# All edge tiles sorted by source block, rows picked by one-hot products, target one-hots made on GpSimd

## The chip, the core and the metric

The kernel runs on one core of one Trainium2 chip. That core has a matrix engine (TensorE, PE in the profile), VectorE (DVE), ScalarE (ACT), GpSimd (POOL), SyncE (SP), which here only starts transfers, and 16 DMA engines. The metric is the device time of one execution in microseconds. The kernel before took 4575.59 us (median of 3 runs, 4570.17 to 4577.93).

## The reference

A graph network on 2500 nodes of 128 features and 82,500 edges, which come sorted by target (`dst`). Six layers of the first kind, cut to what matters:

```
for l in range(6):
    W   = ssp(edge_attr @ mlp_w1[l] + mlp_b1[l]) @ mlp_w2[l] + mlp_b2[l]   # per edge, 100 -> 128 -> 128
    W   = W * C[:, None]                                                  # cosine cutoff of the edge
    xf  = h @ conv_w1[l]                                                  # per node
    msg = xf[src] * W                                                     # row of the edge's source
    agg = segment_sum(msg, dst, num_segments=N)
    x2  = agg @ conv_w2[l] + conv_b2[l]
    h   = h + (ssp(x2) @ lin_w[l] + lin_b[l])
```

Then a layer norm, three layers of the second kind (`agg = segment_sum(h[src], dst)`, then two small products on the nodes), and a layer norm. Everything is float32. `ssp` is softplus minus log 2.

## The kernel before

**Steps.** The edge work goes in groups of 4 tiles of 128 edges, 512 edges a group. One group is one step of the edge loop. A layer has 7 iterations of 24 steps, 168 steps, so the six layers have 1008. In step `i` TensorE runs the first product of group `i` (512 columns into `ps_h`), then the second product of group `i-2` (into `ps_w`), and the aggregation of group `i-4` (into `ps_a`). The groups `i`, `i-2` and `i-4` are thus in the pipe at the same time. ScalarE does exp and log of the first product (`xc`) and fills `ps_w` with the bias (`seed`). VectorE finishes ssp (`hid`), multiplies `ps_w` with the source rows (`message`, written to `ex_msg`), and adds the aggregate into `aggT` (`add_window`).

**Where the source rows come from.** There are two kinds of group. Of every 4 steps, 3 are plain: GpSimd starts 4 indirect DMAs (`gather_group`, one for each tile of 128 rows, from `node_table` in DRAM into `rows`), up to 8 steps ahead. The fourth is permuted: its edges were sorted by source block (20 blocks of 125 nodes) before the layers, so that each tile takes its rows from one block. Its rows come from a product of a 128x128 one-hot (`select`, loaded by DMA) with the block of the node table kept in SBUF (`table`, which shares its space with `hi_mid`). `select_rows` makes that product into `ps_g`, ScalarE copies it to `picked`.

**The target side.** In a plain group the 4 tiles are sorted by target and lie in a window of 32 nodes: one 128x32 one-hot a tile (`hot`), one 128x32 sum and one add. In a permuted group each tile has its own window of 128 nodes: 128x128 one-hots (`phot`, made on VectorE) and four adds, one after the other.

**Counts.** Beside this, VectorE and TensorE count edges by (source, target) for the second kind of layer: 16 count tiles an iteration, placed by `COUNT_STEP`.

**Before the layers.** `rec` holds the records (104 floats an edge) of the 148 tiles that are to be permuted. VectorE computes each edge's place, GpSimd scatters each tile with one indirect DMA into `permuted`, which SyncE has cleared. Then 42 groups are read back, turned by TensorE and written as `attr_permuted` and `src_select`; VectorE makes the 128x128 source one-hots for that (`xc`). The layers start when all are turned.

**After each layer's edges** the last node chunks are updated (`late_chunks`; 3 of the 5 chunks are updated early, within the iterations of `EARLY_AT`), the new table is stored to DRAM, and the next layer starts.

Each engine has its own instruction stream, and semaphores tie them. The order is written out by hand in the loops below.

Of the kernel before, what the change touches and what calls it, by code (L numbers as in the profile page):

```python
# [23 lines left out]
P = 128  # L24
# [9 lines left out]
U = 24  # L34
J = U // M
NIT = 7
BLK = 125
BLOCKS = -(-N // BLK)
NP_GROUPS = NIT * J
NQ_GROUPS = NIT * J * (M - 1)  # L40
REAL = -(-E // GE)
PT = NP_GROUPS * TPG
RT = PT - BLOCKS
QT = -(-E // P) - RT
assert QT <= NQ_GROUPS * TPG
AS, RS = M, 6
assert J * (M - 1) % RS == 0
# [6 lines left out]
EACH = -(-E // P)  # L54
CLEARS, REC_LOADS = 7, 4
REC_STARTS = [c * RT // REC_LOADS for c in range(REC_LOADS)]
# [13 lines left out]
PAD = 2 * TPG  # L70
AHEAD = NCH
LEAD = M
PRIME = 2

EARLY_AT = [3, 5, 6]
EARLY = len(EARLY_AT)
ADD_LAG = 6
COUNT_MAX = 255
LOW = P
RANK_BLOCKS = 3  # L80
# [5 lines left out]
LN_EPS = 1e-5  # L86

# [7 lines left out]
COUNT_STEP = [4, 4, 5, 6, 8, 9, 10, 11, 13, 13, 14, 15, 17, 18, 19, 20]  # L95
# [3 lines left out]
def use_of(u):  # L99
    return u // M * (M - 1) + u % M - 1  # L100


def gathers_of(g):
    return max(0, min(TPG, QT - g * TPG))


def permuted(u):
    return u % M == 0


def gnn_program(nc, xT_d, srcc_d, dst_d, plan_d, ew_d, attr_d, rec_d, edge_w_d, b2_d, first_w_d, node_w_d, gin_w_d,
# [5 lines left out]
    attrp_d = nc.dram_tensor("attr_permuted", [NP_GROUPS, G1, GE], f32, kind="Internal").ap()  # L117
    select_d = nc.dram_tensor("src_select", [NP_GROUPS, P, GE], f32, kind="Internal").ap()
    table_d = [nc.dram_tensor(f"node_table{i}", [NP, F], f32, kind="Internal").ap() for i in range(2)]

    with ExitStack() as ctx:
# [20 lines left out]
        iota = sb("iota", [P, NB * WIN + 1], i16)  # L142
# [18 lines left out]
        cut = sb("cut", [P, NG * TPG])  # L161
        base_f = sb("base_f", [P, NG])
        base_i = sb("base_i", [P, LEAD + NG], i32)
        pbase_f = sb("pbase_f", [P, PT])
        pbase_i = sb("pbase_i", [P, PAD + PT], i32)
        block_i = sb("block_i", [P, PAD + PT], i32)
# [14 lines left out]
        src_all = sb("src_all", [P, NG * TPG], i32)  # L181

        scratch = counts[:, :, :].rearrange("p b n -> p (b n)").bitcast(f32)
        dst_i, src_part, len_raw, len_mask = (scratch[:, i * NG * TPG:(i + 1) * NG * TPG] for i in range(4))
        dst_i, src_part = dst_i.bitcast(i32), src_part.bitcast(i32)
        ends, ends_all, span = (scratch[:, (4 * TPG + 2 * i) * NG:(4 * TPG + min(2 * i + 2, 5)) * NG] for i in range(3))

        TABLES, ALL = (4 * TPG + 5) * NG, (NB + 1) * NCOL // 2
# [4 lines left out]

        rec, at = after(TABLES, RT * REC)
        total, at = after(at, BLOCKS * RT)
# [8 lines left out]
        bucket_shift, at = after(at, BLOCKS)  # L204
        pos_f, at = after(at, RT)
        pos_i, at = after(at, RT)
        slot_i, at = after(at, RT)
        tile_i, at = after(at, RT)
        slot_i, tile_i = slot_i.bitcast(i32), tile_i.bitcast(i32)
        assert at <= ALL  # L210
        rec = rec.rearrange("p (t r) -> p t r", r=REC)
# [4 lines left out]
        bucket = table[:, 0:BLOCKS * RT // 2].bitcast(bf16)  # L216
        src_low = sb("src_low", [P, NG * TPG], i16)
# [16 lines left out]
        buffers = sb("buffers", [P, AS + 2, GE])  # L234
        attr = buffers[0:G1, 0:AS]
        select = buffers[:, AS:AS + 2]
        xT = buffers[:, 0:NCH, :].rearrange("p c n -> p (c n)")
        spare = buffers[:, :, :].rearrange("p c n -> p (c n)")
        above, spare_at = spare[:, 0:(BLOCKS + 1) * RT // 2].bitcast(bf16), (BLOCKS + 1) * RT // 2
# [19 lines left out]
        ex, msg = ex_msg[:, 0:2, :], ex_msg[:, 2:4, :]  # L259

        stage_one, step_one = ex[:, 0, :], ex[:, 1, :]
        hid = sb("hid", [P, 3, GE])
        lg = msg
        picked = hid[:, 2, :]
        kept_attr = [ex[:, 0, :], ex[:, 1, :], buffers[:, 0, :], buffers[:, 1, :]]
# [1494 lines left out]
```

## Time and profile before

| what | value |
|---|---|
| time, median of 3 runs without the profiler | 4575.59 us |
| the profiled execution, from its first to its last instruction (its span; no other time is recorded for it) | 6617.0 us |
| PE busy in the span | 72% |
| PEld, DVE, ACT, POOL busy | 54%, 46%, 33%, 45% |
| mean granted TensorE clock | 0.778 of full speed |
| mean DMA rate | 87 GB/s |
| start of the first `hid`, and of the last one | 376.3 us, 6296.5 us |

"Busy" sums instruction durations by engine. PEld is the loading of weights, which overlaps PE. The granted clock is either full (2.4 GHz) or half (1.2 GHz). "remote" and "another core or an unknown queue" stand for a wait whose end no recorded event explains. The profiled execution is 2041 us longer than the median of the runs.

### The profile page before, as it was taken

To read this page: it belongs to the slowest core of one execution; us is meant where nothing else is said; L and a number is where in the kernel's file an instruction comes from. 1 tells how busy PE (TensorE), PEld (TensorE's weight loads), DVE (VectorE), ACT (ScalarE), POOL (GpSimd) and SP (SyncE) were. 2 spreads that over 40 slices of the span, in tenths; PEclk is the share of its full clock that TensorE was granted. 3 is DMA by queue.
4 is the path that set the end of the run, shared out by engine and by line. 5 is a ranking of instruction groups with operands and counts; after the bars stand their busy time and mean duration, and the time that the engine had idled before them with its cause. 6 is when DMAs were issued, how large, how long until landed. Compare 5 with 4: busy or idle time off the path is not lost.

```text
span 6617.0 us, 88816 instructions
## 1 busy us (share of the span) xinstructions
PE 4785.2 (72%) x24401; PEld 3558.4 (54%) x24684; DVE 3028.4 (46%) x8117; ACT 2174.5 (33%) x3585; POOL 2995.9 (45%) x3161
## 2 busy tenths in 40 slices
PE   0376777867777777777777777767777777777789
PEld 0365555645555555555555555545555555555544
DVE  3244444544444444444444444544444444444532
ACT  0133333333333333333333333333333333333322
POOL 5634444444454445444445444444445444445400
PEclk5687777777777777777777777777778777777799
DMA  4452233233233333233333323233333332323300
GB/s 157 137 151 84 83 86 88 82 91 85 82 87 85 85 90 89 80 86 86 86 86 91 85 84 88 85 85 87 85 85 88 86 89 84 86 84 87 87 14 9
DMA packets 324938, 574.64 MB, mean 87 GB/s; under 512 B 73578, under 2 KB 117300, under 8 KB 322996
## 3 DMA queue, kind: packets, MB, share of 16 engines
q1 hardware_dynamic: 202572, 357.07, 17.9%
q0 software_dynamic: 100160, 203.51, 11.5%
q10 hardware_dynamic: 21928, 11.64, 0.6%
q14 instruction: 261, 2.14, 0.1%
q8 instruction: 17, 0.28, 0.0%
HBM read 524.00 MB, written 47.93 MB: 86 GB/s over the span
## 4 chain that ended last, share of the span: by engine, by line
PE 40%; another core or an unknown queue 27%; issue 13%; DVE 10%; DVEq 4%; ACT 4%; POOL 2%; DMA 1%; ACTq 0%; SPq 0%; POOLq 0%
PE ps_w L680 10%; PE ps_h L781 9%; PE ps_a L695 8%; PE ps_a L692 4%; PE ps_pair L894 3%; POOL permuted L551 2%; DVE ex_msg L1428 2%; PE ps_pair L707 2%; DVEq L342 2%; ACT ps_w L1025 1%; DVE aggT L1409 1%; PE ps_a L669 1%; DVE phot L1388 1%; ACT xc L1062 1%
## 5 line engine op out<-in xcount | busy, mean ns | idle before, releaser
L561 POOL DMA_INDIRECT rows<-node_table,src_all x2982 | 2820.5, 946 | 3117.5 <-DVE ex_msg L1428 1937.8
L680 PEld LDWEIGHTS ps_w<-edge_w,hid 128*128 128x128 f32 x8064 | 1336.7, 242 | 1295.6 <-issue 1295.3
L680 PE MATMUL ps_w<-edge_w,hid 128*128 128x128 f32 x8064 | 1392.8, 329 | 719.0 <-ACT ps_w L1025 471.4
L1571 DVE SCALAR_TENSOR_TENSOR hid<-xc,ps_h 128x512 f32<-128x512 f32 x1008 | 690.9, 686 | 1859.5 <-remote 1328.5
L1060 ACT ACTIVATE xc<-ps_h 128x512 f32<-128x512 f32 x1008 | 601.3, 597 | 2648.2 <-remote 1363.6
L781 PE MATMUL ps_h<-buffers,edge_w 112*128 112x512 f32 x2016 | 1347.9, 756 | 86.4 <-DVE hid L1571 46.3
L695 PE MATMUL ps_a<-hot,ex_msg 128*128 128x32 f32 x6048 | 952.1, 306 | 469.7 <-issue 251.2
L695 PEld LDWEIGHTS ps_a<-hot,ex_msg 128*128 128x128 f32 x6048 | 887.8, 226 | 522.6 <-issue 512.8
L1062 ACT ACTIVATE xc<-xc,half_col 128x512 f32<-128x512 f32 x1008 | 727.3, 722 | 32.6
L1025 ACT COPY ps_w<-seed_rows 128x512 f32<-128x512 f32 x1008 | 591.6, 587 | 413.9 <-DVE ex_msg L1428 342.8
L1416 DVE TENSOR_TENSOR aggT<-aggT,ps_a 128x32 f32 x756 | 140.4, 186 | 927.2 <-remote 631.0
L1428 DVE TENSOR_TENSOR ex_msg<-ps_w,rows 128x512 f32<-128x512 f32 x756 | 518.6, 686 | 0.7
L692 PE MATMUL ps_a<-phot,ex_msg 128*128 128x128 f32 x2016 | 384.7, 351 | 110.0 <-DVE aggT L1416 103.5
L781 PEld LDWEIGHTS ps_h<-buffers,edge_w 112*128 112x128 f32 x2016 | 378.8, 231 | 117.8 <-issue 111.2
L692 PEld LDWEIGHTS ps_a<-phot,ex_msg 128*128 128x128 f32 x2016 | 344.6, 258 | 122.8 <-issue 118.8
L1409 DVE TENSOR_TENSOR aggT<-aggT,ps_a 128x128 f32 x1008 | 290.5, 288 | 209.3 <-issue 64.5
L707 PE MATMUL ps_pair<-pair_hot,low_hot 128*128 128x128 bf16 (+1 forms) x1092 | 284.3, 329 | 114.9 <-DVE pair_hot L1478 48.8
L669 PEld LDWEIGHTS ps_a<-hi_mid,buffers 128*128 128x128 f32 x2016 | 267.7, 193 | 128.4 <-issue 128.4
L1021 ACT COPY hid<-ps_a 128x512 f32<-128x512 f32 x252 | 144.9, 575 | 564.0 <-remote 545.4
L1388 DVE TENSOR_SCALAR phot<-pwin_now,prel_now,pcut_now 128x128 f32<-128x128 f32 x1008 | 283.5, 349 | 0.2
L669 PE MATMUL ps_a<-hi_mid,buffers 128*128 x2016 | 269.8, 277 | 5.2 <-DMA hi_mid<-node_table 3.2
L1478 DVE TENSOR_SCALAR pair_hot<-iota,pair_count 128x640 bf16<-128x640 int16 x672 | 270.2, 402 | 0.0
(236 smaller groups left out, 2825.5 us busy)
## 6 DMA issues: line engine op xcount, KB each, us to landing
buffers<-in_attr SPq DMA_DIRECT2D x756, 224.0 KB
buffers<-src_select SPq DMA_DIRECT2D x252, 256.0 KB
buffers<-attr_permuted SPq DMA_DIRECT2D x252, 224.0 KB
rows<-node_table,src_all POOLq DMA_INDIRECT x2982
permuted<-aggT SPq DMA_DIRECT2D x7, 1248.0 KB, 17.6
hid<-permuted SPq DMA_DIRECT2D x42, 208.0 KB
counts<-in_rec SPq DMA_DIRECT2D x4, 1924.0 KB, 35.4
hi_mid<-node_table SPq DMA_DIRECT2D x6, 1280.0 KB
```

The costliest lines, as they stand in the source:

```text
L561: pool.indirect_dma_start(out=rows[:, use % RS, t * F:(t + 1) * F], out_offset=None, in_=table[:, :], in_offset=bass.IndirectOffsetOnAxis( ...
L669: mm = pe.matmul(ps_g[:, t * F:(t + 1) * F], select[:, u // M % 2, t * P:(t + 1) * P], table[:, bass.ds(starts[t], F)], start=True, stop=True)
L680: mm = pe.matmul(ps_w[u % 2][:, t * F:(t + 1) * F], hid[:, u % 2, t * P:(t + 1) * P], edge_w[:, EW_W2:EW_W2 + F], start=False, stop=(t == ...
L692: mm = pe.matmul(ps_a[:, t * PWIN:(t + 1) * PWIN], msg[:, u % 2, t * F:(t + 1) * F], phot[:, t, :], start=True, stop=True)
L695: mm = pe.matmul(ps_a[:, 0:WIN], msg[:, u % 2, t * F:(t + 1) * F], hot[:, (u % M - 1) * TPG + t, :], start=(t == 0), stop=(t == TPG - 1))
L707: pe.matmul(ps_c[:, first:end], low_hot[:, q % 2, :], pair_hot[:, q % 2, first:end], start=(t == 0), stop=(t == TPG - 1), skip_group_check ...
L781: pe.matmul(ps_h[i % 2][:, :], edge_w[0:G1, EW_W1:EW_W1 + F], attr[:, i % AS, :], start=True, stop=True).then_inc(mm1_done[i % M], 1)
L1025: act.copy(ps_w[v % 2][:, :].rearrange("p (t f) -> p t f", f=F), seed_rows[:, :].unsqueeze(1).broadcast_to([P, TPG, F])).then_inc(seeded[v ...
L1060: act.activation(xc[:, u % 2, :], ps_h[u % 2][:, :], ACT.Exp).then_inc(exp_done, 1)
L1062: act.activation(xc[:, u % 2, :], xc[:, u % 2, :], ACT.Ln, bias=half_col[:, :]).then_inc(log_done[u % M], 1)
L1428: dve.tensor_tensor(msg[:, u % 2, :], ps_w[u % 2][:, :], gathered, ALU.mult).then_inc(msg_done[u % M], 1)
L1571: dve.scalar_tensor_tensor(out=hid[:, i % 2, :], in0=xc[:, i % 2, :], scalar=LOG_MAX, in1=ps_h[i % 2][:, :], op0=ALU.min, op1=ALU.max).the ...
```

## The change

All 645 tiles of 128 edges are now permuted, in three chunks of the target-sorted list (217, 213 and 215 tiles). In each chunk the tiles are sorted by source block, with room for the blocks' last, part-filled tiles: 704 tile slots, 176 groups. A layer is 11 iterations of 16 steps, 176 steps, 1056 in all.

- Every step has a `select_rows` product, a ScalarE copy to `picked` (now two buffers), four 128-node windows and four adds. No indirect DMA is left in the layers; `rows`, `hot`, `rel_now` and `cut_now` are gone.
- The one-hots `phot` (now two buffers) are made by GpSimd, 4 `tensor_scalar` a step, and so are the slices `prel_now` and `pcut_now`.
- SyncE loads `attr` (224 KB) and `select` (256 KB) for every step, 4 buffers each. The node table comes in 5 pieces.
- Before the layers the scatter runs over 645 tiles in 24 parts with 3 record buffers; chunk 1 is turned while chunk 2 is scattered, chunk 2 while chunk 3 is, and chunk 3 after the scatter. 176 groups are turned instead of 42, and `permuted` is cleared in 3 times 13 transfers.
- There are 12 count tiles an iteration instead of 16.

The order on VectorE, one step with its message, around a step without count tiles. Before, the message of a permuted group follows the making of its one-hots, and the adds of a plain group are one:

```order
L1563 UNCONDITIONAL_BRANCH
L1388 TENSOR_SCALAR phot<-pwin_now,prel_now,pcut_now 128x128 x4
L1428 TENSOR_TENSOR ex_msg<-ps_w,hid 128x512
L1571 SCALAR_TENSOR_TENSOR hid<-xc,ps_h 128x512
L1563 COMPARE_AND_BRANCH
L342 ISA
L342 TENSOR_LOAD base_i
L1416 ISA
L1416 TENSOR_TENSOR aggT<-aggT,ps_a 128x32
```

Now (`starts` holds the window starts; the message's rows in `hid` are `picked`):

```order
L336 TENSOR_LOAD starts
L1460 ISA
L1460 TENSOR_TENSOR aggT<-aggT,ps_a 128x128
L1460 ISA
L1460 TENSOR_TENSOR aggT<-aggT,ps_a 128x128
L1460 ISA
L1460 TENSOR_TENSOR aggT<-aggT,ps_a 128x128
L1460 ISA
L1460 TENSOR_TENSOR aggT<-aggT,ps_a 128x128
L393 REGISTER_ALU
L1467 TENSOR_TENSOR ex_msg<-ps_w,hid 128x512
L1599 SCALAR_TENSOR_TENSOR hid<-xc,ps_h 128x512
```

The one-hots have left VectorE, and every step has four 128-column adds.

The order on GpSimd inside the edge loop. Before, gathers alone:

```order
L386 ISA
L561 DMA rows<-node_table,src_all 128x128 x12
L386 REGISTER_ALU
L561 DMA rows<-node_table,src_all 128x128 x8
```

Now, one iteration of 16 steps (its first rows are the slices):

```order
L607 COPY prel_now<-prel 128x64
L608 REGISTER_ALU
L608 COPY pcut_now<-pcut 128x64
L609 ISA
L390 ISA
L592 ISA
L592 TENSOR_SCALAR phot<-pwin_now,prel_now,pcut_now 128x128 x8
L390 REGISTER_ALU
L592 TENSOR_SCALAR phot<-pwin_now,prel_now,pcut_now 128x128 x16
```

The stream of indirect DMAs is replaced by 64 `tensor_scalar` an iteration.

The order on TensorE before, two steps of plain groups with one permuted pick between (`ps_a<-hi_mid,buffers` is the pick from the table):

```order
L781 MATMUL ps_h<-buffers,edge_w 128x512
L680 MATMUL ps_w<-edge_w,hid 128x128 x4
L695 MATMUL ps_a<-hot,ex_msg 128x32 x4
L386 REGISTER_ALU
L781 MATMUL ps_h<-buffers,edge_w 128x512
L337 ISA
L337 TENSOR_LOAD block_i
L404 ISA
L669 ISA
L669 MATMUL ps_a<-hi_mid,buffers 128x128
```

Now, the end of one step and the start of the next:

```order
L709 MATMUL ps_a<-phot,ex_msg 128x128 x4
L813 UNCONDITIONAL_BRANCH
L399 REGISTER_ALU
L795 MATMUL ps_h<-buffers,edge_w 128x512
L336 ISA
L336 TENSOR_LOAD starts
L393 REGISTER_ALU
L689 ISA
L689 MATMUL ps_a<-hi_mid,buffers 128x128
```

The pick stands in every step, and every aggregation is of the wide form.

The diff, cut to its core:

```diff
-U = 24
+U = 16
-NIT = 7
+NIT = 11
+CHUNKS = 3
+CHUNK_GROUPS = [59, 58, 59]
+PARTS, RING = 8, 3
-COUNT_STEP = [4, 4, 5, 6, 8, 9, 10, 11, 13, 13, 14, 15, 17, 18, 19, 20]
+COUNT_STEP = [4, 4, 5, 6, 7, 8, 9, 10, 11, 12, 13, 13]
...
-            for t in range(RT):
-                if t in REC_STARTS:
-                    pool.wait_ge(rec_set, REC_STARTS.index(t) + 2)
-                    pool.sem_inc(gate, 1)
-                pool.indirect_dma_start(
...
+            for r in range(CHUNKS * PARTS):
+                if r % PARTS == 0:
+                    pool.wait_ge(places_set, r // PARTS + 1)
+                    pool.wait_ge(perm_clear, (r // PARTS + 1) * CLEARS * 16)
+                pool.wait_ge(rec_set, r + 1)
+                pool.sem_inc(gate, 1)
+                for t in range(PART_FIRST[r], PART_FIRST[r + 1]):
+                    pool.indirect_dma_start(
+                        out=perm_d[:, :], out_offset=bass.IndirectOffsetOnAxis(ap=pos_i[:, t:t + 1], axis=0),
+                        in_=rec[:, r % RING, t - PART_FIRST[r], :], in_offset=None).then_inc(scattered[r % RING], 16)
...
+            def match(uses, u):
+                uses.wait(agg_done, u - 2)
+                pool.sem_inc(gate, 1)
+                for t in range(TPG):
+                    op = pool.tensor_scalar(phot[:, u % 2, t, :], pwin_now[:, :], prel_now[:, u * TPG + t:u * TPG + t + 1],
+                                            pcut_now[:, u * TPG + t:u * TPG + t + 1], ALU.is_equal, ALU.mult)
+                op.then_inc(phot_done, 1)
...
-                if permuted(u):
-                    select_rows(uses, it, u, layer)
+                select_rows(uses, it, u, layer)
...
                 uses.wait(msg_done, u)
-                if u % M == 1:
-                    uses.wait_permuted(hot_done, u)
+                uses.wait_step(phot_done, u)
                 uses.wait(add_done, u - 1)
                 for t in range(TPG):
-                    if permuted(u):
-                        mm = pe.matmul(ps_a[:, t * PWIN:(t + 1) * PWIN], msg[:, u % 2, t * F:(t + 1) * F], phot[:, t, :],
-                                       start=True, stop=True)
-                    else:
-                        mm = pe.matmul(ps_a[:, 0:WIN], msg[:, u % 2, t * F:(t + 1) * F], hot[:, (u % M - 1) * TPG + t, :],
-                                       start=(t == 0), stop=(t == TPG - 1))
+                    mm = pe.matmul(ps_a[:, t * PWIN:(t + 1) * PWIN], msg[:, u % 2, t * F:(t + 1) * F], phot[:, u % 2, t, :],
+                                   start=True, stop=True)
...
+            def message(uses, u):
+
                 uses.wait(mm2_done, u)
...
+                uses.wait_step(picked_done, u)
+                dve.tensor_tensor(msg[:, u % 2, :], ps_w[u % 2][:, :], picked[:, u % 2, :], ALU.mult
+                                  ).then_inc(msg_done[u % M], 1)
...
+            find_places(0)
+            set_cuts()
+            fill_records(0)
+            fill_records(1)
+            find_blocks(0)
+            fill_records(2)
+            find_places(1)
+            find_blocks(1)
...
+            for r in range(PARTS, CHUNKS * PARTS):
+                fill_records(r)
+                for g in turned_after(r):
+                    turn_group(g)
```

## Rows read from the trace of the kernel before

**Rows 1.** Groups by line on GpSimd (busy us, mean ns of one | idle before, releasers)

```profile
L561 POOL DMA_INDIRECT rows<-node_table,src_all x2982 | 2820.5, 946 | 3117.5 <-DVE ex_msg L1428 1937.8 <-issue 1179.6
L571 POOL PARTITION_ALL_REDUCE buffers<-rows x1 | 1.3, 1291 | 71.1 <-DVE rows L1350 71.1
L539 POOL MEMSET mean_mat<- 128x128 f32 x1 | 0.2, 195 | 0.0
```

**Rows 2.** Timeline of GpSimd: a run of gathers, and the layer's end (start, duration)

```profile
1306.70 0.94 POOL L561 DMA_INDIRECT rows<-node_table,src_all  x1 [0.78 <-DVE ex_msg L1428]
...
1353.87 0.94 POOL L561 DMA_INDIRECT rows<-node_table,src_all  x1 [46.23 <-issue]
...
1371.34 0.94 POOL L561 DMA_INDIRECT rows<-node_table,src_all  x1 [0.30 <-issue]
```

**Rows 3.** One line each: gathers, scatter (ns min/median/max, first and last start)

```profile
L561 POOL DMA_INDIRECT rows<-node_table,src_all x2982: 938/944/1119, 267.6 to 6276.8; - x199
...
L551 POOL DMA_INDIRECT permuted<-counts x148: 954/958/4226, 48.3 to 240.1; - x148
```

**Rows 4.** Waits (engine and line, waited for: us in total, times, longest)

```profile
DVE hid L1571 <- remote: 1328.5, 240, 19.9
```

**Rows 5.** Timeline of VectorE from the layer's last gather (1306.70) to its last `hid`

```profile
1309.89 0.69 DVE L1571 SCALAR_TENSOR_TENSOR hid<-xc,ps_h 128x512 f32<-128x512 f32 x1 [0.51 <-ACT xc L1062]
...
1326.29 0.68 DVE L1571 SCALAR_TENSOR_TENSOR hid<-xc,ps_h 128x512 f32<-128x512 f32 x1
...
1354.01 1.29 DVE L1571 SCALAR_TENSOR_TENSOR hid<-xc,ps_h 128x512 f32<-128x512 f32 x2 [0.89 <-issue]
```

**Rows 6.** Timeline of TensorE: a full-clock step with pick and one count tile

```profile
2395.63 1.10 PE L781 MATMUL ps_h<-buffers,edge_w 112*128 112x512 f32 x2
2396.57 1.05 PE L669 MATMUL ps_a<-hi_mid,buffers 128*128 x8
2397.47 1.06 PE L680 MATMUL ps_w<-edge_w,hid 128*128 128x128 f32 x8
2398.36 0.43 PE L707 MATMUL ps_pair<-pair_hot,low_hot 128*128 128x512 bf16 x2
...
2398.84 1.08 PE L695 MATMUL ps_a<-hot,ex_msg 128*128 128x32 f32 x8
2399.76 1.10 PE L781 MATMUL ps_h<-buffers,edge_w 112*128 112x512 f32 x2
```

**Rows 7.** Timeline of TensorE: an aggregation of the wide form, and what follows

```profile
1482.73 1.34 PE L692 MATMUL ps_a<-phot,ex_msg 128*128 128x128 f32 x8
1483.91 1.02 PE L781 MATMUL ps_h<-buffers,edge_w 112*128 112x512 f32 x2
```

**Rows 8.** Timeline of VectorE in a permuted step: two one-hots of a count tile, four adds, message

```profile
1482.84 0.25 DVE L1477 TENSOR_SCALAR low_hot<-iota,low_count 128x128 bf16<-128x128 int16 x1
1483.00 0.38 DVE L1478 TENSOR_SCALAR pair_hot<-iota,pair_count 128x640 bf16<-128x640 int16 x1
1484.21 1.55 DVE L1409 TENSOR_TENSOR aggT<-aggT,ps_a 128x128 f32 x4 [0.82 <-issue]
1485.67 0.68 DVE L1428 TENSOR_TENSOR ex_msg<-ps_w,rows 128x512 f32<-128x512 f32 x1
```

**Rows 9.** VectorE beside GpSimd's memsets (253) and without them (357, 361)

```profile
253.44 3.10 DVE L1344 TENSOR_SCALAR xc<-iota,hid 128x128 f32<-128x128 int16 x4
...
331.97 0.17 DVE L1341 COPY rows<-hid 128x4 f32<-128x4 f32 x1 [1.62 <-DMA hid<-permuted]
...
361.71 0.17 DVE L1341 COPY rows<-hid 128x4 f32<-128x4 f32 x1 [1.41 <-DMA hid<-permuted]
361.87 0.87 DVE L1344 TENSOR_SCALAR xc<-iota,hid 128x128 f32<-128x128 int16 x4
```

**Rows 10.** Timeline of the scatter beside a long VectorE instruction

```profile
55.95 3.48 DVE L1296 TENSOR_TENSOR buffers<-iota,counts 128x3192 bf16<-128x3192 int16 x1 [0.18 <-issue]
...
56.04 4.23 POOL L551 DMA_INDIRECT permuted<-counts  x1 [0.30 <-issue]
```

More of the change, by code:

```diff
@@ L69 @@
 NB = NP // P
-PAD = 2 * TPG
-AHEAD = NCH
+PAD = 5 * TPG
 LEAD = M
 PRIME = 2
-EARLY_AT = [3, 5, 6]
+STEP_PRIME = 5
+EARLY_AT = [5, 8, 9]
 EARLY = len(EARLY_AT)
+PIECE = BLOCKS // NCH
+assert PIECE * NCH == BLOCKS and all(((c + 1) * PIECE - 1) * BLK + P <= (c + 1) * CH for c in range(NCH))
 ADD_LAG = 6
@@ L1287, in _, with fill_records @@
+            def fill_records(r):
+                first, end = PART_FIRST[r], PART_FIRST[r + 1]
+                part = rec[:, r % RING, 0:end - first, :]
+                dve.wait_ge(rec_in[r % RING], (r // RING + 1) * 16)
+                steps.did(dve.scalar_tensor_tensor(out=part[:, :, COL_LOCAL], in0=block_f[:, first:end],
                                                    scalar=-float(BLK), in1=src_f[:, first:end], op0=ALU.mult, op1=ALU.add))
-                steps.did(dve.tensor_scalar(rec[:, first:end, COL_DST], dst_f[:, QT + first:QT + end], 1.0, None, ALU.add))
@@ L1289, in _ @@
-                steps.did(dve.tensor_copy(rec[:, first:end, COL_CUT], cut[:, QT + first:QT + end]))
+                steps.did(dve.tensor_scalar(part[:, :, COL_DST], dst_f[:, first:end], 1.0, None, ALU.add))
+                steps.did(dve.tensor_copy(part[:, :, COL_CUT], cut[:, first:end]))
                 steps.sync()
                 dve.sem_inc(rec_set, 1)
-            steps.did(dve.memset(cut[:, QT:NQ_GROUPS * TPG], 0.0))
-            after_start = [P, PT, BLOCKS - 1]
-            tile_after3 = tile_after.rearrange("p (t b) -> p t b", b=BLOCKS - 1)
@@ L1299, in _ @@
+            fill_records(4)
+            find_places(2)
+            find_blocks(2)
+            wait_table(dve, 16 * EARLY, 16)
+            dve.memset(ex[:, :, :], 0.0)
+            dve.memset(buffers[:, 0:2, :], 0.0).then_inc(kept_clear, 1)
+            for r in range(5, PARTS):
+                fill_records(r)
             dve.memset(block_i[:, 0:PAD], 0.0)
@@ L1554, in _ @@
                         uses = Uses(dve, n)
[L1555 to L1556 removed]
+                        uses.ready(-1, -5).ready_steps(*range(-5, 0))
                         counted = dve.snap(layer * NIT + it)
@@ L1596, in _ @@
                         if i - 3 < U:
-                            message(uses, layer * K + k, NIT - 1, i - 3)
-                with dve.If(load_early(dve, NIT - 1) > 0):
+                            message(uses, i - 3)
+                with dve.If(load_early(dve, EARLY_AT[-1]) > 0):
                     late_chunks(layer, EARLY)
```

714 lines of the change are left out of this document (353 added, 361 removed).

## The prediction

> **What bounds the kernel now.** I read first the span against the runs: 6617.0 us with the profiler, 4575.6 without. The two differ by 2041 us, so the profiled edge loop can't be read as it stands. The loop is the place: from the first `hid` at 376.3 to the last at 6296.5 the profile has 5920 us for 1008 steps, 5.87 each. The waits say what fills it: VectorE alone waits 1328 us before `hid` for "remote", an end that no event explains, up to 19.9 us at a time [rows 4]. These stretches are gone as soon as GpSimd is idle: its last gather of a layer starts at 1306.70, and from 1309.89 to 1326.29 the last six `hid` follow each other at 16.40 / 5 = 3.28 us [rows 2, 5]. I take them for something that the profiler adds while gathers run.
>
> What is left is GpSimd. Its gathers take 0.94 us and the pause between two is 0.30, whatever the other engines do [rows 2]; over all, 2982 of them take 2820.5 us busy [rows 1]. At 1.249 us, the 2962 within the layers need 3700 us in a row. Add what no gather covers: 376.3 before, five layer changes with 1353.87 - 1306.70 = 47.2 each, less one cadence (46, together 230), and 6617.0 - 6276.8 = 340.2 behind the last gather [rows 2, 3]. The sum is 4646 us, 1.5% above the median of the runs and 1971 below the span. So the runs without the profiler go at GpSimd's cadence: 12 gathers, 15.0 us, for 4 steps, 3.75 a step, with TensorE waiting at times. I make the sum below in terms of this clean time and its parts, and correct it by those 1.5% only where GpSimd's cadence enters.
>
> **The change, part by part.**
>
> *The gathers go.* That takes 3700 us from GpSimd and with it the floor of 3.75 a step. Next is TensorE. A dense step at full clock with a pick and one count tile runs from 2395.63 to 2399.76, 4.13 us: first product 0.94, pick 0.90, second product 0.89, count tile 0.48, aggregation 0.92 [rows 6]. Every step now has the pick, and the aggregation is of the wide form, which takes 1.18 until the next product starts against 0.92 [rows 6, 7]; I take +0.1 of these 0.26, since the long one may hold a wait. A step without count tiles is then 4.13 - 0.48 + 0.1 = 3.75 us, and with 12 count tiles in 16 steps the mean is 3.75 + 0.75 x 0.48 = 4.11. This is TensorE alone, at full clock, with no wait.
>
> *VectorE* loses the one-hots and the `hot` pairs and gains adds. A step is now `hid` 0.69, message 0.68, four adds 1.55, and 0.75 x 0.54 = 0.40 for count one-hots [rows 5, 8]: 3.32. The adds to the counts, the slices of an iteration and the gaps I put at 0.5 (an estimate: these are small instructions that don't change). 3.8 us is just under TensorE's 4.11. In the steps with count tiles (10 of 16) both come close, and the single `ps_a` ties them: an aggregation waits for the four adds of the last, 1.55 us, while TensorE has the next products of 2.73 us to cover it. It is covered, with 1.2 us of room. I add 0.14 a step for the times when the two don't meet: 4.25.
>
> *ScalarE* copies `picked` in each step, a fourth instruction of 0.6 us beside three of 0.6 to 0.7; under 2.6 us of 4.25, hidden. If TensorE were faster, it would still not be next.
>
> *GpSimd's one-hots.* The trace has no such instruction on it. From below: a memset of a 128x128 tile, which only writes, is 0.195 us. From above: 1.25 us, a whole gather with its pause, the costliest thing that it does in a row; the all-reduce of 336 columns is 1.29, or 0.49 for 128 columns [rows 1, 2]. I take 0.45, four are 1.8 us of a 4.25 us step, and they are made a step or two ahead of their use. Cost on the path: nothing. At the upper end four take 5.0 us and set the step (rival 1).
>
> *VectorE against GpSimd.* Beside GpSimd's memsets four small VectorE `tensor_scalar` took 3.10 us, without them 0.87 [rows 9]. That is now a matter of every step: the count one-hots, `dst_hot` and the slices, some 35 instructions an iteration, can each be held behind a one-hot of 0.45. With GpSimd busy for two fifths of the time I expect 0.1 us a step, within the 0.14; at worst 35 x 0.45 / 16 = 1.0 a step. The Trainium skill has the rule for this (SBUF — State Buffer, "Who interferes with whom"): a VectorE instruction that uses two ports, or has two SBUF inputs while GpSimd reads, and a GpSimd instruction exclude each other for their whole length. It speaks against the change. The trace agrees in direction: the same four instructions take 2.2 us more. By the rule `hid`, the message and the adds, with one operand in PSUM, aren't held; if all of the 35 were, the sum would be some 900 us more, if only by chance, 100.
>
> *More steps.* 1056 instead of 1008. At 4.25: 6 x 175 intervals = 1050 x 4.25 = 4463 us.
>
> *Before the layers.* The scatter: 148 instructions from 48.3 to 240.1, 1.264 us each but for one of 4.23 [rows 3, 10]. Now 645: 815 us. It begins later, since the places are computed for 217 tiles instead of 148: were all of the 48.3 us that, they would grow by 0.47 x 48.3 = 23; I take 17, to 65. The 4.23 us fall on a VectorE instruction with two SBUF inputs of 3.48 us [rows 10]; the same work, at larger size, is done for chunks 2 and 3 while the scatter runs, about 22 us of such instructions for each: +45. The scatter ends at 925. Turning: two chunks lie under the scatter (34 us a part for 7.4 groups, where 7.4 x 2.12 = 16 are needed). The third doesn't: 59 groups at (361.71 - 331.97) / 14 = 2.12 [rows 9], 125 us, and 10 more beside the memsets. From the last group to the first `hid` it was 376.3 - 362.7 = 13.6, now 20 with longer rows. First `hid` at 1080, instead of 376: +704. If descriptors cost 1.0 us instead of 1.264 without the profiler, it is 170 less; if the turning is held by DMA beside the scatter, 60 more.
>
> *Layer changes.* From last to first `hid` 1354.01 - 1326.29 = 27.7 [rows 5]; the drain is longer by wide steps: 30, five times 150. The loads of `select` in each step (480 KB in 4.25 us, 113 GB/s) are above the mean of 87 in the profile, but run 3 to 4 steps ahead: no cost; if late, some 0.2 a step. The tail is 320.5, now 324.
>
> *Sum.* 1080 + 4463 + 150 + 324 = 6017 us; with 815 corrected by 1.5%, 6005. Against the clean sum of before, 4646, and the median 4575.6. I forecast 6010 us. The span with the profiler, having no gathers to stall beside, should be near that, below the 6617 of before.
>
> **The rivals.**
>
> 1. *GpSimd's one-hots set the step.* At 1.25 us each (upper end above) a step is 5.0, the layers 5250, the whole 1080 + 5250 + 150 + 324 = 6804. For it: nothing of this kind runs on GpSimd in the trace, and compare and multiply with two scalars is more than a memset. Against: 195 ns for a tile of the same size. The Trainium skill (GPSIMD Engine Reference, "Elementwise — side-by-side cycle accounting") gives 1.03 cycles an element for up to two operations, an estimate of 0.11 us plus some dispatch for 128 columns; by that rule this rival falls, and nothing here shows it yet.
>
> 2. *TensorE doesn't stay at full clock.* At the mean 0.778 of the profile, 4.11 becomes 5.28, and the whole 7100. Against: the half clock comes with the pauses, and the dense steps of rows 6 ran at full rate.
>
> 3. *TensorE alone binds, and the scatter is cheaper.* 4.11 a step is 4316; with no collisions in the scatter the first `hid` is at 1030: 5820.
>
> 4. *Faster than before.* The mechanism: the runs without the profiler too lose their time in waits beside the gathers, and TensorE's steps are shorter than the records. It decides only if a step falls below (4575.6 - 1080 - 150 - 324) / 1050 = 2.88 us. For it: the gathers' own cadence is only inferred for those runs. Against: four products and the first one take 3.65 in rows 6 with nothing between them, and that is a measured start-to-start. Its time, with the first `hid` at 800 (scatters of 0.8 us) and 2.7 a step: 4110.
>
> 5. *The change doesn't do what it says*: tiles spanning over 128 targets would double the passes. From the drawn edges the widest tile spans 101, so one pass remains. No chance.
>
> **How the numbers follow.** Forecast 0.62 (its own range 5850 to 6250), rival 1 0.14, rival 2 0.06, rival 3 0.15, rival 4 0.02, and 0.01 for no change by chance. The range takes in rival 3, the forecast and the part of rival 1 in which a one-hot costs up to 1.1 us: 5650 to 6650. What a measurement can't tell from no change is 0.2%, 9 us; with a distance of 1400 us only rival 4 is on the other side. Faster 0.02, same 0.01, slower 0.97.
>
> **What would show it.** The first `hid` near 1080, the scatter from 65 to 925 with its last third under turning, then 125 us of turning alone. In the layers TensorE busy over 90%, at a granted clock near 1, 4.1 to 4.3 us from `hid` to `hid`, no long "remote". GpSimd's `phot` at 0.3 to 0.6 us. VectorE's count one-hots longer than 0.25 and 0.38. I am wrong if `phot` is over 1 us, if VectorE is what TensorE waits for in most steps (then 4.5 or more), if the first `hid` is below 950, or if the clock falls in the loop.

## The result, and the profile after

The changed kernel takes 6490.5 us (6471 to 6501) where the kernel before takes 4576.8 us (4570 to 4579) on the same chip: a ratio of 1.417, interval [1.414, 1.421]. A run of 7476 us, with a mean clock of 0.71, is left out. Slower, as forecast, inside the stated range of 5650 to 6650, outside the forecast's own range of 5850 to 6250, and 480 us above the 6010.

Parts of the profiled execution (6501.2 us, span 6499.5) against the forecast: first `hid` at 1073.7 (forecast 1080), the intervals within the layers 4919.6 us in all, 4.69 a step (forecast 4463, 4.25), the five layer changes 35.3 to 36.2 each (30), 327.6 from the last `hid` to the end (324). The miss is in the step. "Layers" below is that sum of 1050 intervals between the starts of `hid` instructions, read from the first and last `hid` of each layer.

The busy shares, the granted clock in 40 slices, and the groups that answer to rows 5, 6 and 9 (line, engine, operation, tiles, count | busy us, mean ns | idle before it, and what ended that):

```profile
PE 5331.1 (82%) x34529; PEld 4194.0 (65%) x34530; DVE 3774.4 (58%) x10468; ACT 2761.8 (42%) x4801; POOL 4028.7 (62%) x5030
...
PEclk5576879999999999999999999999999999999999
...
L592 POOL TENSOR_SCALAR phot<-pwin_now,prel_now,pcut_now 128x128 f32<-128x128 f32 x4224 | 3315.9, 800 | 1632.9 <-PE ps_a L709 1601.0
...
L709 PE MATMUL ps_a<-phot,ex_msg 128*128 128x128 f32 x8448 | 1267.4, 296 | 184.0 <-DVE aggT L1460 183.8
...
L1599 DVE SCALAR_TENSOR_TENSOR hid<-xc,ps_h 128x512 f32<-128x512 f32 x1056 | 724.2, 686 | 539.8 <-PE ps_w L699 508.4
```

No `hid` waits for "remote" any more, as against 1328.5 us in the trace of before [rows 4]; it waits for TensorE. GpSimd's one-hot takes 0.80 us, not 0.45, so four are 3.2 us of a step, and GpSimd waits for TensorE 1601 us in all: it isn't the bound. TensorE's waits between 1250 and 6170 us (in total, times, longest):

```profile
PE ps_pair L721 <- DVE counts L1524: 277.4, 128, 2.2
PE ps_a L709 <- DVE aggT L1460: 174.4, 149, 1.8
```

The first line is 128 waits of 2.2 us, two in an iteration (132 in the whole trace, 286 us, each of 2.16 or 2.17). What TensorE waits for is VectorE's add of a finished set of four count tiles into `counts`. VectorE and TensorE around one of them:

```profile
2259.87 0.69 DVE L1599 SCALAR_TENSOR_TENSOR hid<-xc,ps_h 128x512 f32<-128x512 f32 x1 [0.47 <-PE ps_w L699]
2260.47 0.25 DVE L1515 TENSOR_SCALAR low_hot<-iota,low_count 128x128 bf16<-128x128 int16 x1
2260.64 0.38 DVE L1516 TENSOR_SCALAR pair_hot<-iota,pair_count 128x640 bf16<-128x640 int16 x1
2260.93 0.85 DVE L1524 TENSOR_TENSOR counts<-counts,ps_pair 128x672 f32 x1
...
2267.98 0.69 DVE L1599 SCALAR_TENSOR_TENSOR hid<-xc,ps_h 128x512 f32<-128x512 f32 x1 [2.03 <-PE ps_w L699]
```

```profile
2261.93 0.43 PE L721 MATMUL ps_pair<-pair_hot,low_hot 128*128 128x512 bf16 x2 [2.17 <-DVE counts L1524]
2262.29 0.19 PE L723 MATMUL ps_pair<-dst_hot,ones_mat 128*32 128x32 bf16 x1
2262.41 1.21 PE L709 MATMUL ps_a<-phot,ex_msg 128*128 128x128 f32 x8
2263.41 1.92 PE L795 MATMUL ps_h<-buffers,edge_w 112*128 112x512 f32 x2
2265.12 1.86 PE L689 MATMUL ps_a<-hi_mid,buffers 128*128 x8
2266.82 1.05 PE L699 MATMUL ps_w<-edge_w,hid 128*128 128x128 f32 x8
```

The columns of the next rows are the stretch, its length, busy us (x instructions) of PE, PEld, DVE, ACT and POOL, the granted clock, the DMA share and GB/s:

```profile
2259.90:2262.00 2.10, 0.07 (x1) 0.10 (x2) 1.88 (x4) 0.43 (x1) 0.55 (x1) 1.00 0.45 122
2262.00:2263.40 1.40, 1.40 (x11) 1.11 (x11) 0.00 (x0) 0.00 (x0) 0.00 (x0) 1.00 0.44 168
2263.40:2266.80 3.40, 3.40 (x12) 2.36 (x11) 1.80 (x5) 1.32 (x2) 2.98 (x4) 0.50 0.00 0
2266.80:2272.00 5.20, 5.20 (x40) 4.34 (x39) 2.90 (x8) 2.79 (x6) 2.58 (x5) 1.00 0.31 95
```

From `hid` to `hid` this takes 8.11 us instead of 4.13. TensorE stands 2.17 us, and 1.4 us after it has started again 3.4 us pass at a granted clock of 0.50 (1.2 GHz): the first product and the pick take 1.92 and 1.86 instead of 1.02 and 1.05. The clock doesn't fall behind every one of these pauses. In 20 of the 132 the step takes 6.45 us, with the same pause and the clock at 1.00 behind it. One of these, TensorE and the same stretch of 3.4 us:

```profile
2114.83 0.43 PE L721 MATMUL ps_pair<-pair_hot,low_hot 128*128 128x512 bf16 x2 [2.17 <-DVE counts L1524]
...
2116.31 1.02 PE L795 MATMUL ps_h<-buffers,edge_w 112*128 112x512 f32 x2
```

```profile
2116.40:2119.80 3.40, 3.40 (x25) 2.62 (x24) 2.38 (x6) 2.28 (x4) 3.12 (x4) 1.00 0.00 0
```

By step of the iteration, steps 0 to 15, the median intervals are 3.51, 3.54, 4.76, 3.51, 3.90, 4.26, 4.13, 4.13, **8.11**, 4.13, 4.13, 4.13, **8.11**, 4.13, 4.62, 5.35. The two long ones are steps 8 and 12.

Where this comes from: `COUNT_STEP` now has 12 tiles in 16 steps, `6, 7` and `10, 11` at the borders between sets; before it had `6, 8`, `11, 13` and `15, 17`. TensorE makes a tile one step after the number in this list. VectorE adds a finished set of four two steps after the number of its last tile, behind the `hid` of that step. So the set that ends with 6 is added in step 8, and the first tile of the next set, 7, comes in step 8 too and needs that add. Before, that first tile came a step later.

### The profile page after: what moved, and what is told of

It reads as the page before. It is cut to its first block, busy times and chain, and to the rows that moved or that the text cites. A ratio compares the mean times of both kernels' runs of the same rounds, so it can differ in the third digit from the quotient of the medians.

```text
span 6499.5 us, 130502 instructions
## 1 busy us (share of the span) xinstructions
PE 5331.1 (82%) x34529; PEld 4194.0 (65%) x34530; DVE 3774.4 (58%) x10468; ACT 2761.8 (42%) x4801; POOL 4028.7 (62%) x5030
## 4 chain that ended last, share of the span: by engine, by line
PE 66%; POOL 9%; issue 9%; DVE 8%; DVEq 5%; DMA 2%; ACT 1%; SPq 1%; ACTq 0%; POOLq 0%
PE ps_a L709 16%; PE ps_h L795 13%; PE ps_a L689 13%; PE ps_w L699 12%; POOL permuted L574 9%; PE ps_pair L721 4%; DVE aggT L1460 3%; PE ps_pair L908 3%; DVE counts L1524 2%; DVEq L341 2%; PE ps_pair L723 1%; DVEq L336 1%; DVEq L430 1%; DVE hid L1599 1%; DMA hid<-permuted 0%
## 5 line engine op out<-in xcount | busy, mean ns | idle before, releaser
L592 POOL TENSOR_SCALAR phot<-pwin_now,prel_now,pcut_now 128x128 f32<-128x128 f32 x4224 | 3315.9, 800 | 1632.9 <-PE ps_a L709 1601.0
L1460 DVE TENSOR_TENSOR aggT<-aggT,ps_a 128x128 f32 x4224 | 1219.0, 289 | 1155.3 <-PE ps_a L709 598.2
L689 PEld LDWEIGHTS ps_a<-hi_mid,buffers 128*128 128x128 f32 x8448 | 1157.6, 199 | 573.0 <-issue 569.8
L709 PE MATMUL ps_a<-phot,ex_msg 128*128 128x128 f32 x8448 | 1267.4, 296 | 184.0 <-DVE aggT L1460 183.8
L709 PEld LDWEIGHTS ps_a<-phot,ex_msg 128*128 128x128 f32 x8448 | 1082.8, 201 | 229.8 <-issue 120.5
L689 PE MATMUL ps_a<-hi_mid,buffers 128*128 x8448 | 1162.4, 282 | 3.5 <-DMA hi_mid<-node_table 3.5
L574 POOL DMA_INDIRECT permuted<-counts x645 | 654.1, 1014 | 248.1 <-issue 195.4
L1467 DVE TENSOR_TENSOR ex_msg<-ps_w,hid 128x512 f32<-128x512 f32 x1056 | 722.4, 684 | 4.1 <-issue 3.2
L1037 ACT COPY hid<-ps_a 128x512 f32<-128x512 f32 x1056 | 599.0, 567 | 25.8 <-PE ps_a L689 25.0
L721 PE MATMUL ps_pair<-pair_hot,low_hot 128*128 128x512 bf16 (+1 forms) x1584 | 350.3, 303 | 286.0 <-DVE counts L1524 286.0
```

What stands on the lines that cost most here:

```text
L574: pool.indirect_dma_start(out=perm_d[:, :], out_offset=bass.IndirectOffsetOnAxis(ap=pos_i[:, t:t + 1], axis=0), in_=rec[:, r % RING, t - P ...
L592: op = pool.tensor_scalar(phot[:, u % 2, t, :], pwin_now[:, :], prel_now[:, u * TPG + t:u * TPG + t + 1], pcut_now[:, u * TPG + t:u * TPG ...
L689: mm = pe.matmul(ps_g[:, t * F:(t + 1) * F], select[:, u % AS, t * P:(t + 1) * P], table[:, bass.ds(starts[t], F)], start=True, stop=True)
L709: mm = pe.matmul(ps_a[:, t * PWIN:(t + 1) * PWIN], msg[:, u % 2, t * F:(t + 1) * F], phot[:, u % 2, t, :], start=True, stop=True)
L721: pe.matmul(ps_c[:, first:end], low_hot[:, q % 2, :], pair_hot[:, q % 2, first:end], start=(t == 0), stop=(t == TPG - 1), skip_group_check ...
L1460: dve.tensor_tensor(window, window, ps_a[:, t * PWIN:(t + 1) * PWIN], ALU.add).then_inc(part_added[t] if t < TPG - 1 else add_done[u % M], 1)
```

## The experiments

Each kernel was timed in 3 rounds beside the kernel before. The record names the chips of these comparisons (10, 13 and 4), not that of the first. On them the kernel before takes 6629 to 6665 us (medians), not 4577: see the fifth run. The layers of the changed kernel take the same time there (4916.2 in run 5, against 4919.6), so I compare the layers directly, with those of run 5, and whole times by their ratio to the kernel before on the same chip.

**1. The sets of count tiles two steps apart.**

```diff
-COUNT_STEP = [4, 4, 5, 6, 7, 8, 9, 10, 11, 12, 13, 13]
+COUNT_STEP = [4, 4, 5, 6, 8, 8, 9, 10, 12, 12, 13, 13]
```

> The first count tile of a new set of four comes two steps after the last of the set before, instead of one; nothing else changes. Theory (T): in the changed kernel the two steps of each iteration with hid to hid of 8.11 us come from one ordering: TensorE's first tile of a set needs the add to the counts, which VectorE issues behind the hid of the same step. TensorE stands 2.17 us, and after it 3.4 us run at half clock (1.7 us more). Both go: these steps become 4.1, 66 x 2 x 4.0 = 525 us less, 6490 - 525 = 5965. Rival (V): it is VectorE's work for the counts as such (adds of 0.85, one-hots of 0.63), which is only moved by this: at least 6350, with the long steps at other places.

6244.7 us, ratio 0.937 [0.934, 0.939]. Layers 4412 us, 504 less (expected 525); the steps of 8.11 are 4.71 (with two tiles) and the next 3.47; TensorE's wait for `counts` is gone from the list. The whole time isn't the expected 5965, mainly since what stands before the layers takes 1329 us on this chip, not 1074.

**2. The add first in its step.** The loop over `tiles_at(i - 2)` with `add_counts` moves from behind the `hid` to ahead of `add_window`.

> The tiles stay where they are; VectorE's add to the counts is the first instruction of its step instead of the last. T: the add then ends before TensorE comes to the tile, so as in the spaced kernel: 5965, steps of 4.1 to 4.5 us at these two places, no wait of TensorE for counts. V: the same instructions, the same load: at least 6350.

6183.0 us, ratio 0.928 [0.926, 0.930]. Layers 4353 us, 563 less (expected 525); the two steps take 4.13. It also shortens the iteration's last step from 5.35 to 4.26, where the third add stood in the way. Two ways to give the add its time, with the same work on VectorE, take the long steps away, and in run 2 no other step gets longer: the ordering is the cause, V falls.

**3. No counting.**

```diff
-                            for q in tiles_at(i - 1):
-                                count_tile(uses, q)
...
-                            for q in tiles_at(i):
-                                count_hot(uses, q, n)
...
-                                    add_counts(uses, q // TPG, counted)
```

> Leaves out the counting of pairs in the layers (count tiles on TensorE, their one-hots and adds on VectorE; the slices stay), so the output of the last three rounds is not the reference's. T: beside the 525 us of the ordering this takes 12 tiles of 0.6 us from TensorE in each of the 66 iterations, 475 us: about 5490, and every step at 3.5 us except those at the iteration's border. V: about the same, 5450; this run gives the whole price of counting, of which the other two must show how much is the ordering. If the step stays above 4, something beside TensorE and the counting bounds the layers.

5729.6 us, ratio 0.859 [0.857, 0.861]. Layers 3898 us: 1018 less, so counting costs 563 by its order and 455 by its work, 0.57 us a tile. Nearly every step is 3.54 us.

**4. Products into the pause.**

```diff
+                if t == 0 and j:
+                    uses.wait_step(picked_done, u)
+                    keep_turning(8)
                 if t == 0:
                     uses.wait_count(count_added, j - 1)
```

> The changed kernel with its late add, but before TensorE waits for the add it makes 8 idle products of 512 columns (0.21 us each, 1.7 us) whose result is not used. T: the add comes no sooner, so the pause ends when it did, but TensorE has worked through most of it. If the slow products after the pause come from the clock that fell because TensorE stood, they run at full clock: the two steps become 8.11 - 1.8 = 6.3 us, 132 x 1.8 = 238 us less, 6253. Rival (C): the slow products have another cause (the queues or the data arriving late): 6490, or more by the idle products.

6594.9 us, ratio 0.989 [0.987, 0.991]. The two steps take 6.38 (expected 6.3), in all 132 cases, though the tile starts as late as before. The layers take 4727 us, 189 less and not the 238 that I expected: the clock had fallen behind 112 of the 132 pauses only, and 112 x 1.7 is 190. Over 1400 to 6200 us the mean granted clock is 0.99, against 0.95 in the changed kernel. Layer changes are 5 us longer each, which I didn't look into. TensorE in one of these steps, and the clock:

```profile
3235.63 1.91 PE L762 MATMUL ps_a<-still,ones_mat 128*128 128x512 bf16 x8
3237.57 0.45 PE L725 MATMUL ps_pair<-pair_hot,low_hot 128*128 128x512 bf16 x2
...
3239.06 1.02 PE L799 MATMUL ps_h<-buffers,edge_w 112*128 112x512 f32 x2
3239.92 1.06 PE L690 MATMUL ps_a<-hi_mid,buffers 128*128 x8
```

```profile
3235.60:3237.60 2.00, 1.94 (x9) 0.73 (x10) 1.91 (x4) 0.46 (x1) 0.58 (x1) 1.00 0.27 98
...
3239.00:3242.00 3.00, 2.95 (x22) 2.32 (x21) 1.83 (x6) 1.85 (x4) 2.56 (x4) 1.00 0.00 0
```

The products after it are at full clock, C falls: of the 4.0 us that a long step costs, 2.2 are the wait and 1.7 are the clock that fell after TensorE had stood.

**5. The changed kernel once more, on chip 13.**

> The changed kernel itself, unedited, once more beside the kernel before. In the last four comparisons the kernel before took 6651 to 6681 us, not 4570 to 4578, in every one of 7 runs, and the first hid of kernels with the changed kernel's prologue came at 1330 us instead of 1074; the layers kept their times. Theory (S): this belongs to the chip: on one kind ordinary transfers stand still for up to 20 us beside GpSimd's indirect transfers, on the other they don't, with the profiler or without. On a chip where the kernel before takes 6660, the changed one takes 6490 + 257 = 6750 (ratio 1.01); on one where it takes 4576, 6490 (1.42). Rival (P): it is the profiler's doing, as I said in the prediction: the ratio is then 1.42 on any chip.

6734.4 us against 6629.4: ratio 1.016 [1.014, 1.018]. S gives the time to 16 us; P, which is what my prediction says, is false. The kernel before took 6616 to 6692 us in each of its 26 runs on these three chips, so the span of 6617 us in its trace fits such a chip, and its 4576 is that of another. The profiler isn't what makes the stalls either: both traces below are profiled, and only one has them. What S leaves open is what differs. I write "chip with stalls" for short, but the first comparison and the later ones also differ in time, and in whatever else ran beside them; no chip is known to have been measured in both conditions.

On such a chip the changed kernel is 1.6% slower than the kernel before, not 42%. The scatter's instructions (min, median, max ns, first and last start; below it what GpSimd waited for, in us and times), first on the chip without stalls, then here:

```profile
L574 POOL DMA_INDIRECT permuted<-counts x645: 954/959/5591, 62.7 to 912.1; - x162
...
  DVEq L1343: 0.9, 3
```

```profile
L574 POOL DMA_INDIRECT permuted<-counts x645: 956/962/5597, 63.5 to 1154.7; - x162
...
  DVEq L1343: 244.1, 15
```

What all transfers moved between 385 and 425 us, in 40 slices, in the same order, and GpSimd's timeline here:

```profile
GB/s 368 347 254 372 311 318 337 315 253 298 370 400 393 396 408 360 145 80 64 245 247 282 305 323 334 291 257 293 288 279 275 341 328 265 355 383 399 405 402 400
```

```profile
GB/s 53 53 23 216 225 306 147 3 50 53 53 53 0 53 53 53 47 7 53 53 53 0 0 105 239 319 188 347 307 283 303 258 249 316 359 412 378 408 339 234
```

```profile
404.12 0.96 POOL L574 DMA_INDIRECT permuted<-counts  x1 [0.31 <-issue]
421.54 1.03 POOL L574 DMA_INDIRECT permuted<-counts  x1 [16.46 <-DVEq L1343]
```

While GpSimd scatters here, mostly no more than about 50 GB/s move (a scatter carries 128 x 104 x 4 bytes, 53 KB, in 1.26 us): ordinary transfers stand, but for a burst of 4 us from 388. They go on at about 408 (the 24th slice), when GpSimd has stopped for the records of its next part, which are an ordinary transfer too.

**6 and 7. The kernel before with three, and with one, of four gathers.** The tile loop of `gather_group` ends at 3 or at 1, and the waits count as many.

> The kernel before with three of four gathers of a group (the fourth tile of rows is zeros, so the output isn't the reference's). Theory (G): GpSimd's cadence of 1.249 us a gather bounds the kernel before where nothing stands: with 9 gathers for 4 steps it is 11.2 us, below TensorE's 4 x 3.3 = 13.2, which then sets the step: 4576 - 1008 x (3.75 - 3.35) = 4170. On a chip with stalls these go with the number of gathers: 2.1 x 0.75 + 3.35 = 4.9 a step, 5690. Rival (D): it is the time that gathered rows take to land, not GpSimd: less than 100 us gained on either.

> The same with one gather of four (three tiles of rows are zeros; the output isn't the reference's). G: no more to be had than with three of four where there are no stalls, since TensorE sets the step: 4150. With stalls 2.1 x 0.25 + 3.35 = 3.9 a step, 4650. D: in proportion to the gathers, well below 4000 on a chip without stalls. It also gives TensorE's floor for the kernel before.

5638.3 us, ratio 0.851 [0.850, 0.853], and 4526.3 us, 0.683 [0.682, 0.685]. Both are near what G gives with stalls (5690, 4650), and D, which allows 100 us for run 6, falls: it gained 991. Neither was run on a chip without stalls, so G's 4170 and 4150 weren't put to the test there. But with a quarter of the gathers, GpSimd busy for 19% of the time and no stall, a step still takes 3.70 us, not the 3.35 that I put for TensorE, and the whole comes to 50 us below the 4576 of the chip without stalls:

```profile
400.00:4200.00 3800.00, 3537.72 (x22418) 2717.15 (x22418) 2782.50 (x7536) 2006.88 (x3324) 708.63 (x738) 0.97 0.33 94
```

TensorE is busy for 93% of it, so TensorE alone already takes more than G allowed it. The kernel before, where nothing stalls, goes by an estimate at (4576 - 376 - 5 x 27.7 - 320) / 1002 = 3.73 a step (the parts outside the layers are those of its trace), with GpSimd's 3.75 and TensorE's 3.70 side by side: the gathers' cadence isn't a bound that alone hides the rest, as the prediction had it. Which of the two sets the step there isn't shown.

**8. GpSimd without one-hots**, on the kernel of run 1: `match` only counts up `phot_done`.

> The changed kernel with the spaced count tiles, and GpSimd's one-hots left out: phot is zeros, made once (the output isn't the reference's). T: at 0.80 us each they take 3.2 us of a 4.2 us step, next to TensorE, and VectorE's instructions have the same durations as in the kernel before: the step doesn't change where TensorE sets it; only the 66 to 94 us of waits for phot go: 0 to 90 us less than the spaced kernel, which took 0.9365 of the kernel before on its chip. Rival (Q): GpSimd's port use holds VectorE's small instructions, as the prediction feared (up to 1.0 a step): 200 us or more go.

6234.1 us, ratio 0.941 [0.939, 0.943]; layers 4401 us, 11 less. GpSimd's 3.2 us a step are hidden, and VectorE hardly feels them: `hid` takes 685 ns without them and 684 with them, `pair_hot` 382 and 381, `low_hot` 249 and 276. Q falls. The last of these without and with GpSimd's one-hots (run 8, run 1):

```profile
L1513 DVE TENSOR_SCALAR low_hot<-iota,low_count 128x128 bf16<-128x128 int16 x792 | 196.9, 249 | 0.0
```

```profile
L1515 DVE TENSOR_SCALAR low_hot<-iota,low_count 128x128 bf16<-128x128 int16 x792 | 218.5, 276 | 0.0
```

**9. The add first, and the slices in two steps**: the five instructions that work on the slices come in step 3, the three copies stay in step 2.

> The changed kernel with the add to the counts first in its step, and the eight small instructions on the count slices in two steps instead of one. T: what is left of avoidable waits is the step at which TensorE waits 0.9 us for the adds that stand behind these eight; it goes from 4.76 to 3.6 to 3.9, 66 x 1.0 less than the kernel with only the add moved (layers 4353 us): layers 4290. On a chip where the kernel before takes 6650 that is 6120 (ratio 0.92), where it takes 4576, 5860 (1.28). Rival (V): VectorE is that full that the three steps behind pay it back: no change against 4353.

6199.7 us, ratio 0.932 [0.927, 0.937]; layers 4372, no gain over the 4353 of run 2 (expected 4290). Step 2 goes from 4.76 to 3.78, and the next from 3.51 to 4.33. Here my T fails and V holds: the work was only moved.

**10. Half of the scatters.**

```diff
+def sent(r):
+    return [t for t in range(PART_FIRST[r], PART_FIRST[r + 1]) if t % 2]
```

> Sends only every second record tile to its place (the others are left out, so the output isn't the reference's). It measures what the prologue costs by the scatter alone. S with the cadence: 322 scatters fewer, 1.26 us each and half of the stalls: first hid at 1325 - 407 - 125 = 793 on a chip with stalls, 670 to 720 on one without (then turning, 176 groups x 2.12 = 373, is near to binding). Rival (B): the prologue is bound by VectorE's places and by turning, and scatters only run beside it: above 1000.

6344.0 us, ratio 0.953 [0.947, 0.958]; first `hid` at 935, not 793. The first `hid` comes 387 us sooner than in run 5, near the 407 that the cadence gives for 323 scatters fewer. But the stalls don't halve, and there my T fails; GpSimd waits 16 times, 260 us:

```profile
POOL permuted L578 <- DVEq L1347: 260.2, 16, 18.8
```

They come once for a part of records, not once for so many scatters. B falls too, with a first `hid` below its 1000.

**11. Pauses in the scatter.**

```diff
+                    if r >= PARTS and t % 8 == 0:
+                        for _ in range(2):
+                            pauses += 1
+                            pool.memset(idle[:, :], 0.0).then_inc(paused, 1)
+                            pool.wait_ge(paused, pauses)
```

> The changed kernel, in which GpSimd in chunks 2 and 3 makes two memsets of 128x512 after every 8 scatters, 54 pauses of some 1.7 us, 92 us of pauses. Theory (H): on a chip with stalls an ordinary transfer that is under way while GpSimd issues indirect ones lands only when GpSimd pauses: short pauses let it through, the 15 waits of 17 us go, and the first hid comes at 1325 - 250 + 92 = 1170 (time 6580, ratio 0.99); without stalls it comes at 1166 instead of 1074. Rival (K): the stall is a thing of a fixed rate or number, whatever GpSimd does between: 1325 + 92 = 1417, and 6830.

6571.0 us, ratio 0.988 [0.983, 0.993]; first `hid` at 1162.1 (H: 1170). The scatter, made longer by pauses, ends earlier, at 998.5 instead of 1154.7, and the waits for records are gone:

```profile
L582 POOL DMA_INDIRECT permuted<-counts x645: 954/958/5592, 62.7 to 998.5; - x162
...
  issue: 207.3, 625
...
  POOL idle L579: 15.1, 19
```

The breaks came out at 1.9 us between two scatters instead of 0.3. K falls: where ordinary transfers stand beside a GpSimd that issues without a break, a short break lets them through.

**12. Pauses in the gathers of the kernel before.** 16 counts of a semaphore ahead of each group of four.

> The kernel before, in which GpSimd counts up a semaphore 16 times ahead of each group of four gathers, a pause of 1.0 to 1.6 us. Without stalls GpSimd bounds it, so each pause is paid: 756 x 1.3 = 980, 5550 in place of 4576. With stalls, H: ordinary transfers land in the pauses, the step goes from 5.87 to the new cadence of 4.7 to 5.0: 5450 to 5800 in place of 6640, so the slower GpSimd makes it faster. K: 6640 or up to 980 more.

6588.2 us, ratio 0.991 [0.988, 0.994]. It decides nothing: the pause came out at 0.25 us (0.55 between two gathers instead of 0.30), not 1.0 to 1.6, and the step is 5.74 as against 5.77.

```profile
1015.00 0.94 POOL L562 DMA_INDIRECT rows<-node_table,src_all  x1 [0.55 <-issue]
```

That H also holds for the gathers is argued, from the trace of the kernel before and from runs 6 and 7, not shown.

## Why the prediction was right, and where it was off

*The range.* The kernel is slower and the time lies in the range, but not for the reason that the range gives. The part of it above the forecast's own 6250 was there for rival 1, one-hots that set the step, and these are hidden (run 8). That 6490 falls into it is luck. Nor does the upper end follow from its reason: at 1.1 us a one-hot the step is 4.4, and 1080 + 1050 x 4.4 + 150 + 324 = 6174; 6650 stands for 4.85 a step. The distance of 1400 us from the kernel before hung on luck as well: it is that large only where that kernel takes 4577 us, and beside the 6629 of run 5 the changed kernel is 105 us slower.

*What bounds the kernel now.* Two statements fail. The 2041 us between span and median are not the profiler's: the trace and the runs come from two conditions, with stalls and without (run 5). The clean time of 4576 was right as a base only because the comparison fell on a chip without stalls. And GpSimd's cadence is matched by TensorE's own 3.70 us (run 7). The sum didn't suffer, because the cadence was only taken away from it.

*Before the layers:* 1080 against 1073.7, the scatter from 62.7 to 912.1 (65 to 925). The long scatters, of 2.1 to 5.6 us, for which I had put 45 us, cost about 35 (849.4 us from first to last start, against 644 x 1.264 = 814). Nearly all of this lies before 215 us; behind it GpSimd stood at most 0.31 us between two scatters.

*The step, 4.25.* This is the step that failed: "I add 0.14 a step for the times when the two don't meet". The runs split it. TensorE alone was put at 4.11. A step without a count tile takes 3.54 (I had 3.75) and a tile 0.57 (0.48), which makes 3.97. With the order mended (run 2) a step takes 4353 / 1050 = 4.15 with all waits, so the waits that I had in mind are 0.18, near my 0.14, and my 4.25 would have been 0.1 too high. What I put at nothing is another wait of TensorE, 0.54 a step, 563 us: 4.15 + 0.54 = 4.69. It is that of a set's first tile for the add of the set before, which now falls into one step; the `COUNT_STEP` of the diff shows it, and I didn't follow it. Of the 563 us, 504 are the long steps 8 and 12 by run 1: TensorE's waits there are 286, and the slow clock behind them 189 by run 4. The other 59 lie for the most part in the last step of the iteration, where the third add stood in the way (run 2). I had judged the adds to the counts by VectorE's time ("small instructions that don't change"), not by who waits for them. That TensorE alone was put 0.14 too high hid a part of the miss.

*GpSimd's one-hots:* 0.80 against 0.45, within my bounds of 0.195 and 1.25 but above the 0.3 to 0.6 that I named as a sign, and hidden, as said (run 8: 11 us). The rule of the Trainium skill that I set against rival 1 (GPSIMD Engine Reference, "Elementwise — side-by-side cycle accounting", an estimate of 0.11 us for 128 columns, plus a dispatch that I gave no figure) covers a seventh of the 0.80 us; where the rest goes no run here shows. Rival 1 falls by the 0.80 all the same, since it needs over 1.

*VectorE against GpSimd:* I took 0.1 a step; run 8 shows 11 / 1050 = 0.01. The rule of the Trainium skill that I weighed there (SBUF — State Buffer, "Who interferes with whom") would have cost up to 1.0 a step if it had held for all the small instructions; of those that I compared only `low_hot`, 27 ns longer, moves that way.

*Layer changes* 36 against 30, 29 us in all; the tail right. *The clock* stayed at 1.00 in dense steps (0.95 over the layers as a whole), so rival 2 falls; it was lost behind 112 of the 132 pauses of 2.17 us. TensorE was busy for 90% of the layers, as I had said, and this sign didn't show the miss.

*Rival 3* (5820, TensorE alone): with the order mended, 1074 + 4353 + 170 + 328 = 5925 on the chip of the comparison, an estimate from the layers of run 2; it wasn't run there.

*Rival 4*, faster: not on that chip. On one with stalls run 2 is faster than both kernels (0.928 against 1 and 1.016), because the kernel before takes some 2000 us more there, and the changed one 250. That the 2000 are lost beside the gathers follows from runs 6 and 7. Runs 2 and 11 together would be some 160 us less again; this was not run.

## What to carry to other kernels

When a schedule table is made denser, follow for each entry who waits for the result of the last one and where its producer stands in its queue: one step less between the last tile of a set and the first of the next cost 504 us, more than the work of all count tiles (455). Price a wait of TensorE with the slow clock behind it, here 2.2 us of wait and, behind most of them, 1.7 us of clock. And before a gap between a trace and the timed runs is put down to the profiler, ask whether the two come from the same chip and the same conditions.

## What the runs showed of the hardware

- In three comparisons, on chips 10, 13 and 4, ordinary transfers stood for up to 20 us at a time while GpSimd issued indirect transfers every 1.26 us, and moved when it paused; in the first comparison they didn't stand. The kernel before takes 6629 to 6665 us in the three and 4577 us in the first, the changed kernel 6734 (chip 13) and 6490. Whether this goes with the chip or with something else isn't shown.
- After TensorE had stood 2.17 us and worked for 1.4 us, the granted clock was 0.50 for 3.4 us, in 112 of 132 cases (by the length of the step); in the other 20 it stayed at 1.00. Waits of 0.92 and 1.25 us in the same iteration left it at 1.00, and so did 2 us filled with products that nobody reads, in all cases. The two shorter waits, and the stretches behind them:

```profile
2239.57 1.13 PE L709 MATMUL ps_a<-phot,ex_msg 128*128 128x128 f32 x8 [0.92 <-DVE aggT L1460]
...
2302.22 1.02 PE L709 MATMUL ps_a<-phot,ex_msg 128*128 128x128 f32 x7 [1.25 <-DVE aggT L1460]
```

```profile
2240.00:2244.00 4.00, 4.00 (x33) 3.52 (x32) 2.92 (x8) 2.87 (x5) 3.12 (x5) 1.00 0.30 111
...
2304.00:2306.00 2.00, 2.00 (x10) 1.16 (x9) 1.07 (x3) 0.46 (x1) 2.00 (x4) 1.00 0.00 0
```

- A GpSimd `tensor_scalar` with compare and multiply by two per-partition scalars, 128x128, float32, takes 0.78 to 0.80 us (95 of 100) in the changed kernel's trace, four times a memset of that size [rows 1].
